# A graph layer's first gather stage: one basis product for sixteen tiles in place of two for eight

## The reference

```python
W_rel = jnp.einsum('rb,bdf->rdf', w_comp, weight)       # 32 relations, 8 basis matrices
seg = etype * n_nodes + dst
agg = segment_sum(h[src] * norm, seg)                   # per relation and node
node_repr = einsum('rnd,rdf->nf', agg, W_rel) + h_bias + h @ loop_weight
x = layernorm(x + relu(node_repr))
```

## Time and profile before

| what | value |
|---|---|
| median of 3 runs | 3152.14 us (3150.74 to 3162.83) |
| the profiled execution's own time | 3147.97 us |
| its span, first to last instruction | 3146.2 us |
| mean granted TensorE clock | 0.732 of full speed |
| busy: PE, PEld, DVE, ACT, POOL | 2102.7, 1640.2, 1372.2, 621.3, 1602.7 us |
| first gather stage, from PE's first product of it to its last | about 66 to 1254 us of the span |

### The profile page before, as it was taken

One profiled execution on the slowest core, in us unless ns is written; L12 is line 12 of the kernel. 1 busy time (PEld: TensorE's weight loads), 2 busy tenths in 40 slices (PEclk: granted clock), 3 DMA queues, 4 the chain that ended last, 5 costly groups with the idle time before them and its releaser, 6 DMA issues. The chain is left out here.

```text
span 3146.2 us, 45076 instructions
## 1 busy us (share of the span) xinstructions
PE 2102.7 (67%) x11027; PEld 1640.2 (52%) x11028; DVE 1372.2 (44%) x3619; ACT 621.3 (20%) x1018; POOL 1602.7 (51%) x1718
## 2 busy tenths in 40 slices
PE   2656666566666666545666665666665689899996
PEld 2556555565555556423433433333343343399996
DVE  4333333333333333533343333334333367777775
ACT  2111111111111111410010100001001046544443
POOL 5666666656656663246666666666666610090002
PEclk6778787777777877855565566555556579999998
DMA  3222222212122111223333333333333358734442
GB/s 84 56 58 53 59 57 53 59 49 59 53 56 61 51 54 28 87 81 94 95 106 93 95 99 100 97 95 96 101 96 94 96 190 277 235 125 146 149 145 78
DMA packets 131550, 295.74 MB, mean 94 GB/s; under 512 B 35837, under 2 KB 78354, under 8 KB 119200
## 3 DMA queue, kind: packets, MB, share of 16 engines
q1 hardware_dynamic: 73200, 140.32, 13.9%
q0 software_dynamic: 50176, 102.86, 12.7%
q10 hardware_dynamic: 8112, 51.91, 4.2%
HBM read 231.77 MB, written 63.18 MB: 94 GB/s over the span
## 5 line engine op out<-in xcount | busy, mean ns | idle before, releaser
L648 POOL DMA_INDIRECT G<-btab,srcT x784 | 745.1, 950 | 553.6 <-POOLq L56 293.5
L634 POOL DMA_INDIRECT G<-in_x,srcT x784 | 750.5, 957 | 470.4 <-issue 230.5
L834 PE MATMUL PS<-ohT,BIG 80*128 80x512 bf16 x588 | 267.4, 588 | 428.0 <-PEq L56 357.3
L736 PE MATMUL PS<-BIG 128*128 128x192 f32 x1568 | 365.3, 383 | 156.4 <-issue 156.3
L1370 DVE TENSOR_SCALAR ohT<-PS,node_col 80x512 bf16<-80x512 f32 x196 | 145.8, 744 | 712.6 <-DVEq L56 619.9
L736 PEld LDWEIGHTS PS<-BIG 128*128 128x128 f32 x1568 | 323.4, 229 | 192.0 <-issue 191.9
L727 PE MATMUL PS<-BIG,G 128*128 128x192 f32 x1568 | 355.6, 387 | 94.4 <-issue 58.1
L826 PE MATMUL PS<-ident,G 128*128 128x128 f32 x1568 | 379.5, 419 | 5.8 <-PEq L56 4.6
L727 PEld LDWEIGHTS PS<-BIG,G 128*128 128x128 f32 x1568 | 321.9, 232 | 99.9 <-issue 98.9
L954 ACT ACTIVATE BIG<-PS 128x768 f32<-128x768 f32 x196 | 156.8, 811 | 1045.0 <-ACTq L56 900.1
L1216 DVE SCALAR_TENSOR_TENSOR BIG<-PS,dst0T,BIG 128x192 f32<-128x192 f32 x784 | 324.1, 416 | 81.6 <-issue 68.2
(11 more groups left out here) (178 smaller groups left out, 1854.7 us busy)
## 6 DMA issues: line engine op xcount, KB each, us to landing
spill<-BIG ACTq DMA_DIRECT2D x49, 1024.0 KB
BIG<-spill SPq DMA_DIRECT2D x94, 512.0 KB, 5.3
BIG<-spill SPq DMA_DIRECT2D x47, 1024.0 KB, 4.8
G<-in_x,srcT POOLq DMA_INDIRECT x784
G<-btab,srcT POOLq DMA_INDIRECT x784
typ_i<-in_edge_type SPq DMA_DIRECT2D x97, 128.0 KB
BIG<-atab SPq DMA_DIRECT2D x196, 60.0 KB
atab<-BIG SPq DMA_DIRECT2D x12, 384.0 KB
```

The source lines that it names most:

```text
L634: nc.gpsimd.indirect_dma_start(out=G[:, g % 2, t, :], out_offset=None, in_=x, in_offset=bass.IndirectOffsetOnAxis(ap=srcT[:, TPG * g + t:T ...
L648: nc.gpsimd.indirect_dma_start(out=G[:, g % 2, t, :], out_offset=None, in_=btab[:, :], in_offset=bass.IndirectOffsetOnAxis(ap=srcT[:, TPG ...
L736: mm = pe.matmul(PS[:, 4 + p, 0:TPP * TWIN], basis[:, b, :], zs[:, p, :, b, :], start=(b == 0), stop=(b == B - 1), skip_group_check=True)
L834: mm = pe.matmul(PS[:, 2 + k, :], aw[0:WIN, k, a, :], ohT[0:WIN, k % 2, :], start=False, stop=(a == 2), skip_group_check=True)
```

## The change

The basis product is done once a group over all 16 tiles, with 384 columns in place of twice 192. It is done for the group before, after `scaled_sums(h, use, 0)`. `zs` holds two whole groups (slots by group, not by half), so the shared buffer BIG grows from 15 to 18 K elements a partition. The product of group g goes to bank 4 + h. The coefficient lookup moves to bank 7 and behind the loop product, whose signal `loop_ps` is now given by the last lookup matmul in even groups; `scale_coef` moves behind DVE's add of the loop product. DVE's half 1 no longer waits for `seg_ready`: both halves add from the same product, that of group g - 1, and `seg_free` is given once a group. For the last group the two half products stay.

```diff
-        zs = part(2 * TPP * ZW).rearrange("p (s t k n) -> p s t k n", s=2, t=TPP, k=B)
+        zs = part(2 * TPG * ZW).rearrange("p (s t k n) -> p s t k n", s=2, t=TPG, k=B)
...
-                        mm = pe.matmul(PS[:, 4, 2 * P + b * TPC * B:2 * P + (b + 1) * TPC * B], rel_oh[:, b * TILE:(b + 1) * TILE],
+                        mm = pe.matmul(PS[:, 7, 2 * P + b * TPC * B:2 * P + (b + 1) * TPC * B], rel_oh[:, b * TILE:(b + 1) * TILE],
...
-            def basis_product(p, coef_too):
+            def basis_product(h, half=None):
+
+                tiles = slice(0, TPG) if half is None else slice(TPP * half, TPP * (half + 1))
+                bank = 4 + (1 - h if half == 1 else h)
                 take(pe, seg_free)
-                if coef_too:
-                    look_up_coef()
                 for b in range(B):
-                    mm = pe.matmul(PS[:, 4 + p, 0:TPP * TWIN], basis[:, b, :], zs[:, p, :, b, :],
+                    mm = pe.matmul(PS[:, bank, tiles.start * TWIN:tiles.stop * TWIN], basis[:, b, :], zs[:, h, tiles, b, :],
                                    start=(b == 0), stop=(b == B - 1), skip_group_check=True)
                 mm.then_inc(seg_ready, 1)
...
                     scaled_sums(h, use, 0)
                     if not (isinstance(g, int) and g == 0):
-                        basis_product(1, False)
+                        basis_product(1 - h)
                     reached(pe, "pe", x_in[h], 16 * (use + 1))
                     take(pe, loop_done)
                     pe.transpose(PS[:, 7, 0:P], xn[:, h, 0:D], ident[:, :]).then_inc(xwT_ps, 1)
-                    scaled_sums(h, use, 1)
-                    basis_product(0, h == 0 and not last(g, NG))
+                    if last(g, NG):
+                        scaled_sums(h, use, 1, (0,))
+                        take(pe, z_copied)
+                        basis_product(h, 0)
+                    else:
+                        scaled_sums(h, use, 1)
                     take(pe, xwT_ready)
-                    pe.matmul(PS[:, 7, P:2 * P], loop_s[:, :], XT[:, bass.ds(g * TNODES, TNODES)], start=True, stop=True).then_inc(loop_ps, 1)
+                    mm = pe.matmul(PS[:, 7, P:2 * P], loop_s[:, :], XT[:, bass.ds(g * TNODES, TNODES)], start=True, stop=True, skip_group_check=True)
+                    if h == 0 and not last(g, NG):
+                        mm = look_up_coef()
+                    mm.then_inc(loop_ps, 1)
                 by_pairs(pe, NG, one)
+                scaled_sums((NG - 1) % 2, NG // 2, 1, (1,), copied=False)
                 take(pe, z_copied, 2)
-                basis_product(1, False)
+                basis_product((NG - 1) % 2, 1)
...
                     if not first:
-                        starts = firsts_of(dve, before, TPP)
-                        take(dve, seg_ready)
-                        if more and h == 0 and p == 1:
-                            scale_coef(use + 1)
+                        starts = firsts_of(dve, TPG * g - TPG + TPP * p, TPP)
+                        if p == 0:
+                            take(dve, seg_ready)
...
-                            add_tile(starts[j], 1 - p, j)
+                            add_tile(starts[j], 4 + 1 - h, TPP * p + j)
...
-                    if not first:
+                    if not first and p == 1:
                         take(dve, added)
                         dve.sem_inc(added, 1)
                         dve.sem_inc(seg_free, 1)
...
+                    if h == 0 and not last(g, NG):
+                        scale_coef(use + 1)
                     dve.sem_inc(loop_done, 1)
```

More of the change, by code:

```diff
@@ L181, in gnn_kernel @@
         resid = sb("resid", [P, WPB * D])
-        BIG_N = 15 * 1024
+        BIG_N = 18 * 1024
         BIG = sb("BIG", [P, BIG_N])
@@ L718, in _, with scaled_sums @@
             pe.wait_ge(wide_ready, 1)
-            def scaled_sums(h, use, p):
-                take(pe, soh_ready)
-                for c in range(2):
+            def scaled_sums(h, use, p, chunks=(0, 1), copied=True):
+                if 0 in chunks:
+                    take(pe, soh_ready)
+                for c in chunks:
                     k = 2 * p + c
                     reached(pe, "pe", x_gathered[CPG * h + k], 16 * TPC * (use + 1))
-                    take(pe, z_copied)
+                    if copied:
+                        take(pe, z_copied)
                     for q in range(TPC):
@@ L948, in copy_z @@
                 for k in range(CPG):
-                    p, c = k // 2, k % 2
+                    c = k % 2
                     take(act, z_ready)
@@ L953, in copy_z @@
                         act.sem_inc(soh_free, 1)
-                    act.activation(zs[:, p, TPC * c:TPC * (c + 1), :, :].rearrange("p (a q) k n -> p a (q k n)", a=2),
+                    act.activation(zs[:, h, TPC * k:TPC * (k + 1), :, :].rearrange("p (a q) k n -> p a (q k n)", a=2),
                                    PS[:, 2 * c:2 * c + 2, 0:2 * ZW], ACT.Copy).then_inc(z_copied, 1)
@@ L1197, in scale_coef @@
                 step(dve.tensor_tensor(coef[:, tiles, :].rearrange("p (q b) k -> p q b k", q=TPC),
-                                       PS[:, 4, 2 * P:2 * P + TPC * TPR * B].rearrange("p (b q k) -> p q b k", b=TPR, q=TPC),
+                                       PS[:, 7, 2 * P:2 * P + TPC * TPR * B].rearrange("p (b q k) -> p q b k", b=TPR, q=TPC),
                                        nrm, ALU.mult))
@@ L1220, in scaled_hot, with add_tile @@
                     ins.then_inc(soh_ready, 1)
-            def add_tile(at, p, t):
+            def add_tile(at, bank, t):
                 acc = ACC[:, bass.ds(at, TWIN)]
                 take(dve, added)
-                dve.tensor_tensor(acc, acc, PS[:, 4 + p, t * TWIN:(t + 1) * TWIN], ALU.add).then_inc(added, 1)
+                dve.tensor_tensor(acc, acc, PS[:, bank, t * TWIN:(t + 1) * TWIN], ALU.add).then_inc(added, 1)
             def add_messages(wide_tiles):
@@ L1249, in half @@
                 def half(g, h, use, p):
-                    first = isinstance(g, int) and g == 0 and p == 0
-                    before = TPG * g - TPP if p == 0 else TPG * g
+                    first = isinstance(g, int) and g == 0
                     more = not last(g, NG)
@@ L1283, in one @@
                     dve.sem_inc(added, 1)
+                    if h == 0 and not last(g, NG):
+                        scale_coef(use + 1)
                     dve.sem_inc(loop_done, 1)
                 by_pairs(dve, NG, one)
[L1286 to L1289, removed]
+                for p in range(2):
+                    starts = firsts_of(dve, TPG * (NG - 1) + TPP * p, TPP)
+                    take(dve, seg_ready)
+                    for j in range(TPP):
+                        add_tile(starts[j], 4 + (NG - 1 + p) % 2, TPP * p + j)
             for p in range(2):
@@ L1304, in _ @@
             take(dve, added)
-            take(dve, seg_free)
             dve.sem_inc(cb_free, 6)
```

## The result

The changed kernel takes 3130.57 us (median of 7 runs, 3122.60 to 3136.91), the kernel before on the same chip 3155.94 us: ratio of the runs 0.9935, interval 0.9917 to 0.9954. That is 0.65% or 20 us faster; the two medians lie 25 us apart, which is within the interval. The direction was forecast, the size was not: 77 us were, and 3130 lies within the range of 3005 to 3185 us. In the sets of the experiments, single runs of 4555, 6461 and 9049 us stand far from all others and are left out of the ratios. The profiled execution took 3127.32 us, its span is 3125.5 us.

The account below looks back on a forecast made before the run. The prediction took PE's side, slowed in stretches that go with gathers in a row, to set the first gather stage's pace. Its terms, -78 - 64 + 65 = -77 us, gave 3071, or 3075 us as median; range 3005 to 3185.

Parts of the forecast that it names:

- POOL's floor: First gather stage: the least time POOL's list of gathers needs, 982 us in all, against the stage's 1188 us.
- PE's side sets the pace: First gather stage: POOL waits for buffers behind PE's sums and so loses some 230 us.
- First term: Basis product in slow stretches: halving the instructions halves the 156.3 us PE idles before L736, -78 us; bounds none and 156.
- Full-rate part: Basis product in clear stretches: fewer records give nothing, since a 384-column record takes twice the 0.17 us of 192 columns.
- Second term: PE's wait for `loop_done` before the transpose: sums and a double basis product now cover it, -64 us; bounds 0 and 90.
- New waits: PE's added waits in the first stage, for `soh_ready` and `xwT_ready`: together +65 us.
- (a): PE's wait for `soh_ready` of the next group's first half: 22 us in odd groups, 36 us in even ones.
- (b): PE's wait for `xwT_ready` at the loop product, covered by one chunk only: 7 us added, bounds 0 and 40.
- Lookup and coefficients: PE's 24 lookup matmuls keep 27.8 us busy and 82.5 us idle; `scale_coef` delays only `loop_done`, under cover.
- Nothing moves: Rival: slow stretches last until POOL lacks buffers, PE's idle time goes to other lines; 3152 us, chance 0.18.
- Closer to POOL's floor: Rival: slow stretches cost less and PE keeps the high clock more; 3010 us with both terms whole, chance 0.12.
- Slower: Rival: DVE's first half comes late and PE waits for it, mainly in even groups; +32, 3184 us, chance 0.21.

Follow-up runs that it names:

- experiment 6: Changed kernel, but POOL waits in the first stage until each four gathers have landed: ratio to the kernel before 1.1632 (clear set), 1.0586 (stretched set).
- two halves: Changed kernel with each group's basis product split again into two products of 192 columns: 3121.03 us, ratio to the kernel before 0.9967 (stretched set).
- quarter basis: Changed kernel with only 2 of the 8 basis matrices multiplied: 3125.44 us, ratio to the kernel before 0.9903 (stretched set).
- experiment 1: The runs of two halves, the changed kernel with the basis product split again: ratio to the kernel before 0.9967 (stretched set), 0.9989 (first clear set).
- loop late: Changed kernel with loop product and lookup moved behind the next group's first sums: 3216.30 us, ratio to the kernel before 1.0179 (stretched set).
- experiment 8: Both kernels run again unaltered: changed kernel 3123.65 us against 3146.55, ratio 0.9933 (stretched set); the kernel before, profiled again, 3151.10 us.
- Experiment 2: The runs of loop late, the changed kernel with a later loop product and lookup: ratio to the kernel before 1.0179 (stretched set), 0.9989 (first clear set).
- experiment 5: Changed kernel with twenty semaphore increments on POOL's queue ahead of each four gathers: 2665.00 us, one run in a clear set.

## Why the prediction was wrong

**What bounds the stage.** Right that no engine is full and that slow stretches go with gathers in a row (experiment 6 shows it for stretched sets). Right too about POOL's floor: 982 us were worked out (49 x 20.0 is 980), and in a clear set the gathers run from 11.0 to 997.9 us, 987 us. Wrong that all sequencers are slow at once: PE ran 24 matmuls without a gap beside a slow DVE (the result section). The counts of the earlier trace rows also make the contrast look larger than it is, since 37 instructions start in 4 us and the 4 and the 2 in 2 us each. Wrong: "PE's side sets the pace". Taking 576 matmuls from PE gave 10 us, taking half of DVE's adds 14. What stays nearly the same in the stretched sets is POOL's wait for buffers, 231, 225, 234 and 224 us in the kernel before, the changed one, two halves and quarter basis. A clear set has 56 (two halves, 53.0 and 3.0), all of it the ordinary 0.30 us between gathers, so no real wait. The likely reading is a cycle: gathers in a row slow the other queues, buffers run out, POOL stops, the rest catch up in the pause, and POOL starts the next row. A shorter list of PE then is worked off in the pause all the same. That is argued from the rows above; no run shows it by itself, and what makes a queue slow stays open.

**First term, fewer instructions: -78 forecast, about -10 measured** (experiment 1). This is the step that failed. The idle time ahead of L736 was taken as a price per record of that line, and it was halved. The runs show that this idle time is not a price of the line's records: with half of them it nearly vanished from the line and came back at others, and the kernel gained 10 us. That it belongs to a stretch of time set by POOL's row of gathers is the likely reading. The bound "none (the idle time only moves to the next instruction)" was named, and it was nearly what happened: 5.4 us are left ahead of L739, and L729 has 175 us more.

**Full-rate part.** Right: 384 columns cost about twice 192. A group of 16 takes 5.32 to 5.53 us in the timeline, at a granted clock of 0.96 to 1.00, where 16 of 192 took 2.76 at 1.00. In clear sets the basis product is busy 297.7 us with 1568 records (two halves) and 277.2 with 768 (loop late), and the kernels take the same time.

**Second term, `loop_done`: -64 forecast.** The idle time ahead of the transpose fell by 28 us, of which the semaphore's part is 64.0 to 53.5 (in the second pair of profiles, experiment 8, by 47 us, from 110.4 to 63.2). The cover of sums and double basis product is as long in columns in two halves, and there the wait is gone: 4.5 us. There PE idles 60 us inside the basis product instead, ahead of the wait. So this wait can go without the time going with it; it should not have been summed as a gain of its own.

**New waits: +65 forecast.** (a) The wait at L729 by PE's queue rose from 27.9 to 109.7, with 7.8 by DVE's L1227: +90 where 58 was summed. In the second pair of profiles the same two waits go from 44.2 to 87.7, +44, so the 58 lie between two measurements, and this part was not clearly wrong. The queue's part also holds waits for `z_copied` and for gathers, which the trace doesn't tell apart. (b) `xwT_ready`: 32.2 to 130.7, +98 where 7 was summed; above its bound of 40 as well. The second pair has +95. The product had lost half its cover; that a slow ACT (104.5 us idle by "issue" ahead of its copies in this stage) then shows at once is the likely reason. Experiment 2 shows that this wait can't simply be covered: it cost 78 us to take away.

**The order as a whole.** -64 + 65 = +1 was forecast, and experiment 1 measured -10. The sums are close, but by luck: the transpose gave 28 us of idle time where 64 were forecast, and the loop product and the sums took 188 where 65 were. What moved to them from the basis product is in no term of the prediction.

**Lookup and coefficients.** Forecast: their idle time stays. It went to 0, since the lookup now stands right behind the loop product, which takes the wait. `scale_coef` has 11.8 us of idle time before it in its new place, 72.5 in the old one.

**The rivals.** "Nothing moves" told the mechanism best: stretches last until POOL runs out of buffers, and idle time goes to the next line. It was given 0.18, and its 3152 us miss by the some 20 us that the two parts give. It rested on the sight of an even group idling at several lines in turn, and that was better evidence than the total ahead of L736. "Closer to POOL's floor" named the right floor, but no part of this change reaches it. "Slower" did not come about: PE's wait at L729 is 117.5 us, under the 140 given as its sign. Loop-late shows that a bad order can cost 78 us in a stretched set, but not that it does so by this rival's chain.

**The signs.** 768 records of 384 columns: yes. Their mean duration is 523 ns in place of 383, 1.4 times and not twice; records overlap (one of 192 columns alone is 0.32 to 0.48 us long, and a gapless row has one in 0.17), and only the pace of a gapless row is twice. Half of 156 us ahead of L739: no, 5. Idle ahead of the transpose down to 25: no, 62. POOL's semaphore waits down to 150: no, 225. Even groups shorter by 2 to 4 us: by 5.5, but the odd ones are 5.2 us longer. "Wrong if the idle time before L727 and L712 grows by as much as that before L736 shrinks": L727 and L712 together went from 176.9 to 269.4, +92 of the 151, and the loop product took the rest.

## What to carry to other kernels

Idle time that ends by "issue" may belong to a stretch of time, and not to the line it stands before. Before pricing an edit by it, ask what ends the stretch, and suppose that the idle time goes to the next line: what is left then is the safe part of the gain. If several engines are slow in one stretch, look for the one that isn't, and for what stops it. And look whether they are slow at the same moments. A kernel should be measured in more than one set: here the kind of set is worth 480 us and the edit 20.

## What was not expected of the hardware

- The same kernel takes 2670 or about 3150 us, by set, and each set keeps to its level: its 7 to 29 runs of the kernel before stay within 1% of each other, but for the one of 4555 us. In clear sets a long row of gathers slows nothing: the first stage takes 956 us, and POOL's list of gathers 946 (experiment 8).
- In stretched sets the queues of PE, DVE and ACT can be slow. In the first stage of the changed kernel PE has 150.9 us of idle time by "issue" ahead of its sums, DVE 282.7 ahead of its adds, ACT 104.5 ahead of its copies; in a clear set (two halves) it is 0, 0 and 0.8. PE turned slow 8.7 us into one row of 16 gathers, DVE 5.7 us into the row before, where PE ran on. The first stage loses no time to it when the row is broken by pauses of 2.4 us after each four: 1380 us in both kinds of set (experiment 6). No run here tells what makes the queues slow.
- A gather of 0.95 us lands 2.5 us after its start (median, experiment 6). A wait for the last of four left POOL idle for 2.4 us, so the next gather starts some 0.8 us behind the landing; a wait for the third left it idle for 1.1 to 1.6.
- Twenty semaphore increments on POOL's queue ahead of each four gathers made no pause: the gathers stayed 0.30 us apart (experiment 5).
